# First norm shared with ScalarE, and small work moved into the sort, in a two-layer graph kernel

## The reference

```python
edge_index = jnp.stack([src, dst])
h = jnp.maximum(_layernorm(x, axis=-1), 0.0)
x = x + _L0_gnn_ref(h, edge_index, node_vec, gate_w1, gate_w2, msg_w1, msg_w2)   # sums over edges by src
h = jnp.maximum(_layernorm(x, axis=-1), 0.0)
x = x + _L1_gnn_ref(h, edge_attr_64, edge_weight, node_vec1, node_vec1_n2,
                    prob_w, review_score_w, review_w, src, dst)                  # sums over edges by dst
```

## Time and profile before

| what | value |
|---|---|
| median of 3 runs | 5860.72 us (5858.96 to 5861.17) |
| the profiled execution's own time | 5850.4 us |
| its span | 5848.8 us |
| busy: TensorE, VectorE, ScalarE, POOL | 74%, 80%, 45%, 60% of the span |
| chain that ended last, by engine | PE 46%, POOL 16%, issue 13%, DVE 12%, DMA 7%, ACT 4% |

### The profile page before, as it was taken

One profiled execution on the slowest core, in us unless ns is written; L12 is line 12 of the kernel. 1 busy time (PEld: TensorE's weight loads), 2 busy tenths in 40 slices (PEclk: granted clock), 3 DMA queues, 4 the chain that ended last, 5 costly groups with the idle time before them and its releaser, 6 DMA issues.

```text
span 5848.8 us, 116279 instructions
## 1 busy us (share of the span) xinstructions
PE 4353.4 (74%) x25010; PEld 2800.9 (48%) x25010; DVE 4655.6 (80%) x10137; ACT 2612.1 (45%) x6383; POOL 3493.6 (60%) x3689
## 2 busy tenths in 40 slices
PE   6214999999999999999999999545555555455455
PEld 4213555555555555555555555334444444444444
DVE  9887988989889898898988989756666666666665
ACT  4103777777777777777777777510000000000000
POOL 1002656656566665666656566367777777777776
PEclk9657999999999999999999999855555555555555
DMA  6501333333333333333333333322322322322322
GB/s 245 132 0 48 81 78 78 81 78 78 80 78 79 79 78 79 80 77 80 79 78 81 78 78 80 97 72 56 59 56 56 60 56 56 60 56 56 60 56 51
DMA packets 459109, 437.02 MB, mean 75 GB/s; under 512 B 268369, under 2 KB 340274, under 8 KB 457906
## 3 DMA queue, kind: packets, MB, share of 16 engines
q0 software_dynamic: 122512, 173.81, 17.2%
q1 hardware_dynamic: 308706, 249.41, 15.2%
q10 hardware_dynamic: 27840, 13.23, 1.3%
HBM read 363.27 MB, written 72.83 MB: 75 GB/s over the span
## 4 chain that ended last, share of the span: by engine, by line
PE 46%; POOL 16%; issue 13%; DVE 12%; DMA 7%; ACT 4%; SPq 1%; ACTq 1%; DVEq 0%; POOLq 0%
PE ps_hidden L1782 9%; PE ps_beta L1834 9%; POOL work L853 8%; POOL ends L853 8%; PE ps_hidden L1783 7%; PE ps_beta L1842 7%; DMA ends<-src_table,src_quads 5%; PE ps_alpha L1816 4%; DVE work L1450 4%; DVE work L1317 4%; PE ps_sum L1853 3%; ACT beta_scaled L949 3%; PE ps_T L1771 3%; PE ps_alpha L1825 2%; DMA attn_quads<-in_edge_weight 1%
## 5 line engine op out<-in xcount | busy, mean ns | idle before, releaser
L751 POOL DMA_INDIRECT ends<-split_table,src_pairs x1612 | 1579.5, 980 | 1573.8 <-issue 1422.3
L1317 DVE TENSOR_TENSOR work<-work,ps_hidden 128x512 f32<-128x512 f32 x1612 | 1102.8, 684 | 25.6 <-ACT work L897 6.7
L1782 PE MATMUL ps_hidden<-ends_parts,w_high 128*128 128x512 f32 x2418 | 1063.7, 440 | 60.7 <-DVE work L1317 58.8
L897 ACT ACTIVATE work<-ps_hidden 128x512 f32<-128x512 f32 x1612 | 960.5, 603 | 62.6 <-PE ps_hidden L1783 33.9
L1783 PE MATMUL ps_hidden<-ends_hot,window 128*128 128x512 f32 x2418 | 952.6, 394 | 0.0
L853 POOL DMA_INDIRECT work<-src_table,src_quads x808 | 763.2, 945 | 313.4 <-issue 219.3
L853 POOL DMA_INDIRECT ends<-src_table,src_quads x804 | 759.2, 944 | 245.0 <-issue 223.9
L2006 PE MATMUL ps_beta<-work,dst_rows_sb 128*128 128x128 f32 x1608 | 416.4, 441 | 564.0 <-DVE work L1713 564.0
L1115 ACT ACTIVATE ps_alpha<-dots 128x8 f32<-128x8 f32 x403 | 72.6, 180 | 1673.3 <-DVE dots L1675 1673.3
L1834 PE MATMUL ps_beta<-work,msg_w_sb 128*64 128x512 f32 x3224 | 804.2, 609 | 0.4 <-DVE work L1317 0.2
L2006 PE MATMUL ps_beta<-work,equal 128*128 128x128 f32 x1616 | 417.2, 440 | 511.3 <-DVE work L1713 511.3
(11 more groups left out here) (204 smaller groups left out, 6650.1 us busy)
## 6 DMA issues: line engine op xcount, KB each, us to landing
window<-window_table SPq DMA_DIRECT2D x403, 192.5 KB
parts<-in_edge_attr SPq DMA_DIRECT2D x101, 512.0 KB
dst_rows_sb<-by_src SPq DMA_DIRECT2D x403, 128.0 KB
ends<-split_table,src_pairs POOLq DMA_INDIRECT x1612
window_table<-parts SPq DMA_DIRECT2D x49, 386.0 KB, 2.4
sums<-key_rows POOLq DMA_DIRECT2D x403, 32.6 KB
work<-src_table,src_quads POOLq DMA_INDIRECT x808, 2.4
ends<-src_table,src_quads POOLq DMA_INDIRECT x804, 2.4
```

What stands on the lines that cost most here:

```text
L751: pool.indirect_dma_start(out=ends[m][:, t, :], out_offset=None, in_=split_table, in_offset=bass.IndirectOffsetOnAxis(ap=src_pairs[m // 2] ...
L897: nc.scalar.activation(scaled[k % NL][:, :], ps_hidden[k % NL][:, :], ACT.Copy, scale=SLOPE).then_inc(scaled_ready, 1)
L1317: nc.vector.tensor_tensor(hidden[k][:, :], scaled[k % NL][:, :], ps_hidden[k % NL][:, :], ALU.max).then_inc(hidden_ready, 1)
L1782: nc.tensor.matmul(o, w1_high[:, k * P:(k + 1) * P], ends_parts[j][:, :], start=True, stop=False)
```

## The change

The sum over each row stays on VectorE; squares with their sum move to ScalarE, one instruction a tile (49), scaled so that the square is of (sum - 64 x); the variance and the shift are small VectorE operations after the 4th and 5th pass of the sort. ScalarE applies the norm as a Relu with scale and shift, one instruction a tile, in chunks of seven: chunks 0 and 1 before the projection, chunks 2 to 6 within it, after the low copies of tiles 0, 4, 8, 12 and 16. VectorE splits chunk 0 after the 8th pass, chunk 1 after the 9th, and one more every six passes. TensorE's `turn_column` waits for the chunk it reads. The far weights' split moves from behind turn 0 to the head of turn 1; offsets and reach move to the heads of turns 2 to 6. POOL's tail copies wait for the squares, which use the same memory. Between the layers the first of the two head additions becomes `add_pairs` and stands ahead of the variance.

In the diff, the lines of offsets and reach that leave their old place are the same as the added ones and are cut to the first.

```diff
@@ -778,6 +778,7 @@
                     add_rows(quad - 1, 2 * m - 3)
 
             pool.wait_ge(tail_step, 2)
+            pool.wait_ge(sqrt_out, NT)
             for t in range(NT):
                 if t >= 2:
@@ -887,9 +888,19 @@
                 for k in range(5):
                     act.dma_start(flat[:, k * ZW:(k + 1) * ZW], zeros).then_inc(done, 16)
 
+            act.wait_ge(x_in, 16)
             act.wait_ge(sqrt_in, 1)
+            for t in range(NT):
+                nc.scalar.activation(first_squares[:, t, :], x_sb[:, t, :], ACT.Square, bias=stat[:, 0, t:t + 1],
+                                     scale=-float(D), accum_out=stat[:, 1, t:t + 1]).then_inc(sqrt_out, 1)
+            act.wait_ge(sqrt_in, 2)
             nc.scalar.activation(stat[:, 2, :], stat[:, 1, :], ACT.Sqrt).then_inc(sqrt_out, 1)
 
+            def first_norm(c):
+
+                for t in range(c * CH, (c + 1) * CH):
+                    nc.scalar.activation(centered[:, t, :], x_sb[:, t, :], ACT.Relu, bias=shift[:, t:t + 1],
+                                         scale=stat[:, 3, t:t + 1]).then_inc(sqrt_out, 1)
 
             def scale_chunk(b, k):
@@ -1019,16 +1030,21 @@
             act.wait_ge(made, 7)
             nc.scalar.activation(less[:, :], ident[:, :], ACT.Copy, scale=-1.0).then_inc(less_ready, 1)
             nc.scalar.activation(w1_high[:, :], w1_far[:, :], ACT.Copy).then_inc(w_high_ready, 1)
+            act.wait_ge(sqrt_in, 3)
+            first_norm(0)
+            first_norm(1)
             copy_column(0)
             copy_column(1)
             copy_high(0)
             for t in range(NT):
                 copy_low(t)
+                if t % 4 == 0 and t // 4 + 2 < NCH:
+                    first_norm(t // 4 + 2)
                 if t + 2 < NT:
                     copy_column(t + 2)
                 if t + 1 < NT:
                     copy_high(t + 1)
-            act.wait_ge(parts_split, 2)
+            act.wait_ge(parts_split, 2 * NCH)
             act.wait_ge(step, STEPS_TABLE0)
             act.dma_start(nodes(split_table)[:, :, 0:D], h_parts[0]).then_inc(tables_split, 16)
@@ -1182,31 +1198,39 @@
             for m in range(4):
                 link(nc.vector.memset(terms_quad[m][:, :, W0 - 1:W0], 1.0))
 
-            def norm():
-
-                def wide(k):
-                    return stat[:, k, :].unsqueeze(2).broadcast_to([P, NT, D])
-                link(nc.vector.tensor_reduce(out=stat[:, 0, :], in_=x_sb[:, :, :], axis=AX.X, op=ALU.add))
-                link(nc.vector.tensor_scalar(stat[:, 0, :], stat[:, 0, :], 1.0 / D, None, ALU.mult))
-                link(nc.vector.tensor_tensor(centered[:, :, :], x_sb[:, :, :], wide(0), ALU.subtract))
-                link(nc.vector.tensor_tensor(first_squares, centered[:, :, :], centered[:, :, :], ALU.mult))
-                link(nc.vector.tensor_reduce(out=stat[:, 1, :], in_=first_squares, axis=AX.X, op=ALU.add))
-                nc.vector.tensor_scalar(stat[:, 1, :], stat[:, 1, :], 1.0 / D, EPS, ALU.mult, ALU.add).then_inc(sqrt_in, 1)
-                dve.wait_ge(sqrt_out, 1)
-                link(nc.vector.reciprocal(stat[:, 3, :], stat[:, 2, :]))
-                link(nc.vector.tensor_tensor(centered[:, :, :], centered[:, :, :], wide(3), ALU.mult))
-                link(nc.vector.tensor_scalar(centered[:, :, :], centered[:, :, :], 0.0, None, ALU.max))
-
             dve.wait_ge(x_in, 16)
-            norm()
-            nc.vector.tensor_copy(h_parts[0].bitcast(F32R), centered[:, :, :]).then_inc(parts_split, 1)
-            dve.wait_ge(parts_split, 1)
-            nc.vector.tensor_tensor(h_parts[1], centered[:, :, :], h_parts[0], ALU.subtract).then_inc(parts_split, 1)
+            nc.vector.tensor_reduce(out=stat[:, 0, :], in_=x_sb[:, :, :], axis=AX.X, op=ALU.add).then_inc(sqrt_in, 1)
             dve.wait_ge(loaded, 16 * LOADS)
             link(nc.vector.tensor_copy(table_sb[:, :, D:D + 1], pos_sb[:, :].unsqueeze(2)))
-            assert LAYER0_STEPS[0] == STEPS_TABLE0
-            dve.wait_ge(near_high_ready, 1)
-            nc.vector.tensor_tensor(near_parts[1], w1_near[:, :], near_parts[0].bitcast(F32), ALU.subtract).then_inc(near_low_ready, 1)
+
+            def first_variance():
+
+                dve.wait_ge(sqrt_out, NT)
+                nc.vector.tensor_scalar(stat[:, 1, :], stat[:, 1, :], 1.0 / D ** 3, EPS, ALU.mult, ALU.add).then_inc(sqrt_in, 1)
+
+            def first_shift():
+
+                dve.wait_ge(sqrt_out, NT + 1)
+                link(nc.vector.reciprocal(stat[:, 3, :], stat[:, 2, :]))
+                assert LAYER0_STEPS[0] == STEPS_TABLE0
+                nc.vector.scalar_tensor_tensor(out=shift[:, :], in0=stat[:, 0, :], scalar=-1.0 / D, in1=stat[:, 3, :],
+                                               op0=ALU.mult, op1=ALU.mult).then_inc(sqrt_in, 1)
+
+            def split_near_weights():
+
+                dve.wait_ge(near_high_ready, 1)
+                nc.vector.tensor_tensor(near_parts[1], w1_near[:, :], near_parts[0].bitcast(F32),
+                                        ALU.subtract).then_inc(near_low_ready, 1)
+
+            def split_chunk(c):
+
+                at = slice(c * CH, (c + 1) * CH)
+                dve.wait_ge(sqrt_out, NT + 1 + CH * (c + 1))
+                nc.vector.tensor_copy(h_parts[0][:, at, :].bitcast(F32R), centered[:, at, :]).then_inc(parts_split, 1)
+                dve.wait_ge(parts_split, 2 * c + 1)
+                nc.vector.tensor_tensor(h_parts[1][:, at, :], centered[:, at, :], h_parts[0][:, at, :],
+                                        ALU.subtract).then_inc(parts_split, 1)
+
             dve.wait_ge(made, 7)
 
...
@@ -1384,27 +1408,6 @@
                                     ALU.min).then_inc(firsts_ready, 1)
             nc.vector.tensor_scalar(first_node[:, :], dst_all_sb.rearrange("p (w e) -> p w e", e=T)[0:1, :, 0], NP - WIN, None,
                                     ALU.min).then_inc(fits_step, 1)
-            dve.wait_ge(firsts_spread, 1)
-            nc.vector.tensor_tensor(offset[:, :].rearrange("p (w e) -> p w e", e=4 * T), dst_fours,
...
@@ -1459,9 +1462,63 @@
                     order_pairs(pairs_of_way(1 - of, d, run, 1, length)[::-1], pairs_of_way(of, d, run, 1, length), turned)
                 return 1 - of
 
+            def offsets_of_targets():
+
+                dve.wait_ge(firsts_spread, 1)
+                nc.vector.tensor_tensor(offset[:, :].rearrange("p (w e) -> p w e", e=4 * T), dst_fours,
+                                        ps_sum[:, 0:NB].rearrange("p (w a) -> p w a", a=4)[:, :, 0:1]
+                                        .broadcast_to([P, NB // 4, 4 * T]), ALU.subtract).then_inc(fits_step, 1)
+
+            def steps_of_quads():
+
+                quad_firsts = ps_sum[:, 0:NB].rearrange("p (w a) -> p w a", a=4)[:, :, 0]
+                nc.vector.memset(carry_at[:, 0:1], 0.0).then_inc(carry_step, 1)
+                nc.vector.tensor_copy(carry_from[:, :], quad_firsts[:, 0:NQ - 1]).then_inc(carry_step, 1)
+                dve.wait_ge(carry_step, 2)
+                nc.vector.tensor_tensor(carry_at[:, 1:NQ], quad_firsts[:, 1:NQ], carry_from[:, :], ALU.subtract).then_inc(carry_step, 1)
+
+            def furthest_offset():
+
+                dve.wait_ge(fits_step, 3)
+                nc.vector.tensor_reduce(out=reach[:, 1:2], in_=offset[:, :], axis=AX.X, op=ALU.max).then_inc(fits_step, 1)
+
+            def nearest_offset():
+
+                nc.vector.tensor_reduce(out=reach[:, 2:3], in_=offset[:, :], axis=AX.X, op=ALU.min).then_inc(fits_step, 1)
+
+            def reach_of_quads():
+
+                dve.wait_ge(carry_step, 3)
+                nc.vector.tensor_reduce(out=reach[:, 7:8], in_=carry_at[:, :], axis=AX.X, op=ALU.min).then_inc(carry_step, 1)
+                dve.wait_ge(carry_step, 4)
+                dve.wait_ge(fits_step, 5)
+                nc.vector.tensor_tensor(reach[:, 2:3], reach[:, 2:3], reach[:, 7:8], ALU.min).then_inc(carry_step, 1)
+                nc.vector.tensor_tensor(carry_at[:, :], spare[:, 0:1].broadcast_to([P, NQ]), carry_at[:, :], ALU.subtract).then_inc(carry_step, 1)
+                dve.wait_ge(carry_step, 6)
+                nc.vector.tensor_scalar(carry_at[:, :], carry_at[:, :], float(NP), None, ALU.subtract).then_inc(carry_step, 1)
+
+            def split_far_weights():
+
+                dve.wait_ge(w_high_ready, 1)
+                for j in range(2):
+                    nc.vector.tensor_tensor(window[j][0:D, 0:HID], w1_far[0:D, :], w1_high[0:D, :].bitcast(F32),
+                                            ALU.subtract).then_inc(w_low_ready, 1)
+
             def turn_runs(n, k, inward, of):
 
                 assert TURNS[n] == (k, inward, of, sorted_by[0])
+                if n == 1:
+                    split_far_weights()
+                elif n == 2:
+                    offsets_of_targets()
+                elif n == 3:
+                    steps_of_quads()
+                elif n == 4:
```

(34 more changed lines are left out.)

18 lines of the change are left out of this document (removed).

## The result

The changed kernel takes 5874.96 us (median of 12 runs, 5869.53 to 5880.15) against 5859.91 us (12 runs, 5858.5 to 5861.17): a ratio of 1.0026, with a 95% interval of 1.0018 to 1.0033. It is slower by 15.05 us on the medians; 17.7 were forecast. Its profiled execution took 5877.71 us with a span of 5876.1, which is 27.3 more than the span before.

What follows compares the result with a forecast made beforehand. ScalarE's queue of DMA issues was taken to end the sort's first turn, nearly tied with VectorE. +22.7 there and -5.0 between layers gave +17.7 on 5850.4, 5868.1; with the median's 10.3 carried over, 5878.4; range 5862 to 5888.

Steps and rivals of the forecast that it cites:

- VectorE's head start: Sort in the first stage: begins 20.6 us earlier, but this ends in waits for TensorE, then ScalarE.
- the hold: ScalarE's seven DMA issues before its bank copies at the first turn: 33.1 us, kept unchanged; bounds 0.6 and 33.1.
- Rival 1: ScalarE's queue: issues now cost little, the hold goes away, TensorE decides; 12.3 us less, 5848.4; chance 0.10.
- the pass after the turn: Sort's first pass after turn 0, its first turn: at 235.5 instead of 212.77, +22.7 us.
- VectorE's start: First pass of the sort at 28.6 instead of 49.19, with loads in at about 21.6.
- The start of the projection: First columns wait for chunk 0's split: starts at 49.5, 12.8 us later; bounds 12.5 and 15.
- The three new waits: VectorE's waits for ScalarE before the projection starts: 15 us later instead of 12.8 if each costs 0.7.
- The norm inside the projection: Five chunks on ScalarE's path, in steps of 5.1 us instead of 2.8: 11.7 us; bounds 0 and 12.2.
- Rival 2: Projection: the norms fit in gaps while ScalarE waits for TensorE; sum falls to +6.0, 5866.7; chance 0.12.
- the work moved into the turns: Far split, offsets and two reductions in turns 1 to 6, covered by VectorE's waits; uncovered they would cost 8.4 us.
- Between the layers: Addition of pairs fills VectorE's idle gap ahead of the variance in five chunks: -5.0 us; bounds 0 and -5.5.

Runs made afterwards that it cites:

- run 2: Changed kernel with the seven table and zero stores issued by SyncE instead of ScalarE: 5830.63 us, ratio 0.9962.
- run 5: Changed kernel with norms of chunks 2 to 6 spread, two tiles after each of the projection's first 18 tiles: 5864.98 us, ratio 1.0019.
- run 4: Changed kernel with all seven chunks of norm ahead of the projection, none within it: 5861.48 us, ratio 1.0012.
- run 9: Kernel before with seven tiny VectorE memsets added ahead of the loop, on the third chip: 6843.09 us, ratio 0.9998.
- run 7: Changed kernel with the addition of pairs put back behind the variance between the layers: 5875.05 us, ratio 1.0036.
- run 1: Changed kernel again, unedited: 5872.06 us against 5854.15, ratio 1.0029.
- run 8: Kernel before again, unedited, a single execution on another chip than the unedited changed kernel's: 5852.27 us.
- run 6: Kernel before with only offsets, reach and the far weights' split moved to the heads of turns 1 to 6: 5853.51 us, ratio 0.9999.
- run 12: Changed kernel, stores on SyncE, all norms before projection; variance, shift, near split before sort; chunk 0 split after pass 6: 6811.14 us, ratio 0.9953, third chip.

## Why the prediction was right, and where not

**Direction and mechanism: right.** The time is inside the range, 3.4 us under the forecast; that it came so near is in part luck, as the terms below show. The forecast said that VectorE's head start would end in two waits, for TensorE and then for ScalarE, and that ScalarE's issues, moved by the projection's later end, set the turn. The rows show both waits, and run 2 shows the cause: without the hold the loss of 17.9 us becomes a gain of 23.5 against the kernel before. Rival 1 put the pass after the turn at 205.5 us in that case; it came at 206.45. What rival 1 had wrong was its premise: the issues do not become cheap. Its total, 12.3 us under the kernel before, also lacked the loop's 8.4 us and the longer hold of ordinary executions; 23.5 were measured.

**VectorE's start: right in size.** 28.6 forecast, 29.40 measured; the loads landed 0.75 us later.

**The start of the projection: right.** +12.8 forecast, +13.0 measured at the first copy. The three new waits cost nothing together: the sort's rows run on without a gap, since ScalarE had its part ready each time.

**The norm inside the projection: right as a term, incomplete as a stage.** A step with a norm took 5.13 us against 5.1. But the stage was summed as five steps at 5.1 and the others at 2.81, on the unspoken premise that TensorE runs as fast behind a gap of 2.7 us as without. The first store was to be issued 24.5 us later and was 31.4. The missing 6.9 us are the five slow tiles, 7.8, less 0.9 that the first chunk hides in the first step (6.50 us, where that step takes 5.05 in the trace of before). Run 5 gives the 11.7 us of the forecast exactly, with no such tile, and run 4 gives nothing, with no norm there. Rival 2, that the norms fit in gaps, is refuted by the same 11.7 and by every step of 5.12. Its opposite, that a gap costs more than its length, was not among the rivals and should have been.

**The hold: mis-sized.** 33.1 us was carried over unchanged; it measured 39.8. Part of this is scatter of the kernel before itself (33.2, 36.2 and 37.2 in three traces, and 31.9 in run 9 on the third chip), part belongs to the changed kernel: 38.0 to 40.7 in all its traces with these stores on ScalarE. The part that belongs to it lies in the second table store. It took 11.0 to 13.7 us in the seven traces in which it was issued while VectorE still sorted its runs, and 14.5 to 16.3 in the seven in which the sort had ended, whichever engine issued it; the five stores of zeros show no such split (19.4 to 23.7). Those seven are also the ones in which it was issued after 195 us. What makes it longer was not tried, and stays open. The rule of the Trainium skill cited ahead (DMA: Bandwidth & Descriptors, section Issuing engines are not separate DMA queues), that initiating a DMA is usually small beside the DMA itself, fails again here: the second table store holds ScalarE for 16.24 us of the 42.7 from its issue to its landing (11.85 of 36.2 before), the stores of zeros for 22.82 us, and what stands behind them in its program waits.

**The pass after the turn**: +22.7 forecast, +36.2 measured, 13.6 us too little, from the two terms above (6.9 and 6.7). From there on to the first gather the shift is kept (+36.7), so the work moved into the turns is covered, as forecast.

**Between the layers: right.** -5.0 forecast, -4.8 measured in the two profiles and 4.9 in run 7.

**The loop of layer 0: a term that was missing.** The forecast took it as untouched, and it gave 8.4 us: VectorE's pause of 0.10 us once in each of some 100 rounds is gone, and seven operations more ahead of the loop are enough to take it away (run 9). This offset more than half of the error above. The sum of landmarks is +36.7 - 8.4 - 4.8 + 3.8 = +27.3, the last term being the second layer's loop, 2033.7 us in this trace but 2029.4 in that of run 1, so scatter. Set against run 8 (another chip, with a kernel before within 0.3 us of this one's), run 1 has +34.8 at the gather and +22.0 at the end; its execution lay 2.3 us above its median and run 8's 1.6 under that of the kernel before, which leaves +18.1, beside the +17.9 of the medians. The forecast of +17.7 is therefore nearer than its terms deserve: at the turn it has 13.6 us too little, in the loop 8.4 too much, and that the two errors offset each other is luck. Part of the rest is that the profiled execution of before lay 9.5 us under its median, some 3 of them in the very hold that the sum rests on, to judge by the holds of 36.2 and 37.2 us in runs 8 and 6.

**The bound that was missing.** The hold's bounds went from 0.6 to 33.1, with the one measured value as upper end; a value seen in one execution is no bound.

## What to carry to other kernels

DMA issues that block an engine for tens of us belong on an engine whose next instruction nobody waits for; before giving a loaded engine a head start, look at what its first rendezvous waits for on the other engines, for there the head start ends, and each later arrival there is paid in full. When work is put into the gaps of a pipeline that TensorE runs at full clock, put it in pieces small enough that TensorE does not stand still for long, or ahead of the pipeline: here 35 activations cost 7.7 us ahead of it, 11.7 in it by twos (one trace), and 13.7 to 20.8 in lumps of seven (four traces). Take a stall's duration from more than one execution before it becomes a term. When a loop whose code was not touched changes by a constant amount a round, look within the round: whole times could not tell 0.10 us that two rows show.

## What the hardware showed that was not expected

- TensorE's granted clock fell from 1.00 to 0.50 behind the third chunk inside the projection in the profiles of the changed kernel and of runs 1 and 7, and not in run 2, whose third chunk begins at 84.65 us, against 84.69 in run 1, with the same gap for TensorE. A 128x512 product took 0.79 us instead of 0.50. What decided between the two was not found; in runs 1 and 2, and not in the other two, the clock also fell behind the first chunk (the stretch at 0.52 shown in run 2). In all four traces with chunks of seven inside the projection the clock fell there at least once, and in none of the other ten. A stretch of run 1 behind the third chunk:

```profile
90.00:95.00 5.00, 4.62 (x17) 3.47 (x16) 4.93 (x11) 2.17 (x6) 0.19 (x1) 0.50 0.42 158
```

- The issue of the second table store, 6272 rows of 65 values, holds ScalarE as long as SyncE (11.85 and 12.65 in the kernel before, 16.24 and 16.30 in the changed one). Its length is not the change's alone: in run 12, which has the change and issues it while VectorE still sorts, it took 10.97.
- Identical code in layer 0's loop ran at 31.75 us a round in six traces and at 31.85 in four. The 0.10 us are one pause of VectorE between two operations, at the same place of every round, and seven tiny operations far ahead of the loop take it away (run 9). Other numbers of operations were not tried.
- The 16 DMA engines stay busy through the whole hold: their busy share is nine tenths or more in 37 of its 40 equal slices, in the kernel before (177 to 210 us) and in the changed one (209 to 248). Whether the issuing engine stands because of this was not tried.
